# Row maxima of self attention: joined per 128 queries and sent by transfers of 4-byte pieces, in place of a transpose per block

## The reference, cut to what matters

```python
scores = jnp.einsum('bqhd,bkhd->bhqk', q, k) / np.sqrt(HD)
attn = jax.nn.softmax(scores.astype(jnp.float32), axis=-1)
out = jnp.einsum('bhqk,bkhd->bqhd', attn, v)
```

## Time and profile before

| | us |
|---|---|
| median of 3 runs | 3796.76 (3792.34 to 3797.68) |
| the profiled execution, its own time | 3797.3 |
| its span in the trace | 3795.5 |

### The profile page before, as it was taken

The page is one execution under the profiler, slowest core; times in us unless marked ns, Lnnn a source line. Parts: engine busy times, 40 slices in busy tenths (PEclk is TensorE's granted clock), DMA queues, the critical chain, the costliest instruction groups (busy, mean ns, idle before and its releaser), DMA issues.

```text
span 3795.5 us, 59346 instructions
## 1 busy us (share of the span) xinstructions
PE 3443.8 (91%) x22289; PEld 2023.6 (53%) x22289; DVE 2237.3 (59%) x3533; ACT 2316.6 (61%) x4047; POOL 830.5 (22%) x546
## 2 busy tenths in 40 slices
PE   8999998898999888998898889988998899899988
PEld 6777776434644564446435744465446443564465
DVE  3323324885386556953885559636955487549654
ACT  2333333786577645875786557765874578657764
POOL 0322323003400521024003410051014100340051
PEclk8989989999999999999999999999999999999999
DMA  5001002000000001001000010000000100000000
GB/s 173 7 29 34 6 31 89 1 13 24 27 2 1 13 15 53 2 24 38 2 2 13 12 56 2 24 24 16 2 13 12 56 1 13 24 27 2 7 18 13
DMA packets 73089, 87.17 MB, mean 23 GB/s; under 512 B 11823, under 2 KB 62578, under 8 KB 72694
## 3 DMA queue, kind: packets, MB, share of 16 engines
q1 hardware_dynamic: 47846, 63.23, 5.1%
q10 hardware_dynamic: 24976, 20.15, 1.7%
HBM read 72.49 MB, written 9.56 MB: 22 GB/s over the span
## 4 chain that ended last, share of the span: by engine, by line
PE 76%; DVE 13%; ACT 7%; issue 2%; POOL 1%; DMA 0%; SPq 0%; ACTq 0%; DVEq 0%; POOLq 0%
PE ps L677 71%; DVE mxh L1721 4%; ACT probs L1406 3%; PE ps L1122 3%; DVE ctxk L1670 2%; DVE ow L1746 1%; PE ps L983 1%; DVE tok L1456 1%; DVE x L1687 1%; DVE small L1440 1%; DVE mx L1718 1%; ACT qs L1373 1%; POOL hidl L1832 1%; POOL small L1768 1%; ACT ow L1412 1%
## 5 line engine op out<-in xcount | busy, mean ns | idle before, releaser
L1406 ACT ACTIVATE probs<-ps 128x512 f32<-128x512 f32 (+1 forms) x2176 | 1216.5, 638 | 290.3 <-PE ps L677 247.7
L1721 DVE TENSOR_REDUCE mxh<-ps 128x2 f32<-128x1024 f32 x1024 | 1212.7, 1220 | 155.8 <-PE ps L677 152.7
L677 PE MATMUL ps<-probs,v 128*32 128x256 f32 (+2 forms) x7616 | 727.9, 454 | 6.3 <-ACT probs L1406 6.3
L677 PE MATMUL ps<-ks,qs 64*128 64x512 f32 x2048 | 483.1, 480 | 63.7 <-DVE mxh L1721 45.3
L1768 POOL TENSOR_TENSOR small<-small 128x4 f32<-128x4 f32 x66 | 67.8, 1027 | 2012.8 <-DVE small L1450 2012.8
L677 PE MATMUL ps<-qs,ks 64*128 64x512 f32 x2048 | 455.6, 425 | 4.0 <-DVE mxh L1721 2.5
L677 PEld LDWEIGHTS ps<-ks,qs 64*128 64x128 f32 x2048 | 192.8, 183 | 424.8 <-issue 302.0
L677 PEld LDWEIGHTS ps<-qs,ks 64*128 64x128 f32 x2048 | 248.1, 186 | 184.1 <-ACT probs L1406 150.1
L677 PEld LDWEIGHTS ps<-probs,v 128*32 128x32 f32 (+1 forms) x7616 | 150.2, 108 | 275.8 <-ACT probs L1406 204.6
L677 PE MATMUL ps<-hT,slot 128*128 128x512 f32 x448 | 233.5, 654 | 21.8 <-issue 8.5
L1718 DVE TENSOR_REDUCE mx<-ps 128x4 f32<-128x312 f32 x384 | 166.2, 478 | 146.2 <-PE ps L677 142.8
(11 more groups left out here) (221 smaller groups left out, 5919.2 us busy)
## 6 DMA issues: line engine op xcount, KB each, us to landing
slot<-in_L_w SPq DMA_DIRECT2D x8, 1024.0 KB, 10.0
slot<-in_L_fc_w SPq DMA_DIRECT2D x8, 1024.0 KB, 5.4
xin<-in_x ACTq DMA_DIRECT2D x5, 1024.0 KB, 6.1
x_after_block<-x ACTq DMA_DIRECT2D x20, 256.0 KB, 2.4
xin<-x_after_block SPq DMA_DIRECT2D x5, 1024.0 KB, 5.5
ew<-in_L_e_w SPq DMA_DIRECT2D x6, 768.0 KB, 14.3
x<-in_x ACTq DMA_DIRECT2D x4, 1024.0 KB, 6.9
qs<-mrow SPq DMA_DIRECT2D x256, 2.0 KB
```

The lines of the kernel that those rows point to most:

```text
L677: return pe.matmul(out, lhsT, rhs, start=start, stop=stop)
L1406: ins = act.activation(dst, src, ACT.Exp, scale=SCALE)
L1721: dve.tensor_reduce(mxh[:, z, t, j // 2, j % 2, :], ps[:, a:a + 2, :], AX.X, ALU.max, negate=True).then_inc(dve_done, M.add(dve_done, name))
```

## The change

The join now works on one query block: `both` has a step for each t, with 128x4 results in place of 128x16, and stands one A behind the last reduction of its t. Behind each join SP waits for it and issues four transfers, one per head, which take one column of `mx` (128 partitions, 4 bytes each) to 512 consecutive bytes of one partition of `qs`. The transpose M, ScalarE's copy and the four transfers of 512-byte runs are kept for the first block (0, 0) of each module only, and dropped for the other seven. The joins of the third block wait for the kept M, and from the fourth block on a block's first join waits for the transfers of the block two before it (they read the same half of `mx`); ScalarE's wait for transfers goes. Wait counts on `maxima_stacked` grow with the number of transfers.

```diff
     def self_attention(tag, follow):
-        maxima, turn = [], []
+        maxima, last = [], []
         for g in range(GROUPS):
             for n in range(NH):
-                scores = [("A", g, n, t, j) for t in range(TPH) for j in range(GH)]
-
-                behind = 1 if (g, n) == (0, 1) else 4
-                maxima += turn[:1] + scores[:behind] + turn[1:] + scores[behind:]
-                turn = [("both", g, n), ("M", g, n)]
-        maxima += turn
+                for t in range(TPH):
+                    maxima += [("A", g, n, t, 0)] + last + [("A", g, n, t, j) for j in range(1, GH)]
+                    last = [("both", g, n, t)]
+                if (g, n) == (0, 0):
+                    maxima += last
+                    last = [("M", g, n)]
+        maxima += last
...
+                        if KIND[tag] == "self" and (g, n) != (0, 0):
+                            for t in range(TPH):
+                                sp.wait_ge(dve_done, upto(dve_done, (tag, "both", g, n, t)))
+                                at_column = n * HALF + t * P
+                                for j in range(GH):
+                                    sp.dma_start(qs[stacked(j % 2, MAXROW, MAXROW + 1), 2 * g + j // 2, at_column:at_column + P].bitcast(F32),
+                                                 mx[:, z, 0, TPH * j + t:TPH * j + t + 1]
+                                                 ).then_inc(maxima_stacked[g][n], M.add(maxima_stacked[g][n], (tag, j - GH + 2) if t == TPH - 1 else None, LOADED))
+                            continue
...
-                        if not cross and NH * g + n >= 2:
-                            act.wait_ge(maxima_stacked[g - 1][n], upto(maxima_stacked[g - 1][n], (tag, 1)))
...
-                        g, n = step[1:]
+                        g, n, t = step[1:]
                         z = maxima_of(tag, g, n)[0]
-                        if NH * g + n >= 2:
-                            dve.wait_ge(mm_done, upto(mm_done, (tag, "M", g - 1, n)))
-                        dve.wait_ge(dve_done, upto(dve_done, (tag, "A", g, n, TPH - 1, GH - 1)))
-                        dve.tensor_tensor(mx[:, z, 0, :].rearrange("p (c e t) -> p t c e", t=TPH, e=2), mxh[:, z, :, :, 0, :], mxh[:, z, :, :, 1, :], ALU.min
-                                          ).then_inc(dve_done, M.add(dve_done, (tag, "both", g, n)))
+                        if (g, n) == (1, 0):
+                            dve.wait_ge(mm_done, upto(mm_done, (tag, "M", 0, 0)))
+                        elif NH * g + n > 2 and t == 0:
+                            dve.wait_ge(maxima_stacked[g - 1][n], upto(maxima_stacked[g - 1][n], (tag, 1)))
+                        dve.wait_ge(dve_done, upto(dve_done, (tag, "A", g, n, t, GH - 1)))
+                        dve.tensor_tensor(mx[:, z, 0, :].rearrange("p (c e t) -> p t c e", t=TPH, e=2)[:, t], mxh[:, z, t, :, 0, :], mxh[:, z, t, :, 1, :], ALU.min
+                                          ).then_inc(dve_done, M.add(dve_done, (tag, "both", g, n, t)))
```

More of the change, by code:

```diff
@@ L1062, in _ @@
                         pe.wait_ge(act_done, upto(act_done, *act_was))
-                        last = (tag, "A", GROUPS - 1, n, TPH - 1, 0) if cross else (tag, "both", g, n)
+                        last = (tag, "A", GROUPS - 1, n, TPH - 1, 0) if cross else (tag, "both", g, n, TPH - 1)
                         pe.wait_ge(dve_done, upto(dve_done, last, *dve_was))
```

## The result

The change made the kernel slower: 3806.09 us, median of 20 runs (3791.15 to 3811.55), against 3792.39 for the kernel before in the same comparison. The ratio is 1.0038, with a 95% interval of 1.0027 to 1.0050. One of the 20 executions of the kernel before took 6517.69 us and is left out of the ratio; the others took 3781.46 to 3797.73. The forecast was 3764 us and faster, with a range that ended at 3779, so size, range and sign were all wrong. The changed kernel's profiled execution took 3810.91 us with a span of 3809.0, which is 13.5 us more than the span before, at a mean granted TensorE clock of 0.956 where before had 0.961.

The account below looks back on a forecast made before the run. TensorE was taken as the bound, busy 91%. Per module 2.6 + 1.8 - 0.3 = 4.1 us, times 8 modules 32.8 us, off the profiled 3797.3 gave 3764.5, forecast as 3764 us; range 3754 to 3779.

Parts of the forecast that it names:

- Added: joins on VectorE: Four joins per block in place of one: hidden in the stream, 0.3 us per module ahead of it, bounds 0 and 0.8.
- Removed, in the stream: Six transposes between later A matmuls go: 0.43 us each, 2.6 us per module, bounds 1.3 and 2.6.
- Removed, at the end: The transpose behind the last A and its join goes: S comes earlier, 1.8 us per module, bounds 0 and 2.27.
- Transfers: 112 new transfers replace 28 per module: SP keeps up, issue and landing hidden, 0.9 us in hand at the last block.
- rival (a): The last block's transfers land late and take back the end's 1.8 us: 3778 us; chance 0.13 with other part losses.
- 4-byte pieces: Each t sends 512 pieces into one or two partitions; needs 10.2 ns or less each, 8.3 taken, so nearly free.
- rival (c): Pieces into one partition above 10.2 ns delay each block's first S: 3845 to 4135 us; chance 0.08 with anything else slower.
- (b): VectorE becomes the bound in the stream if a join costs 0.35 us or more: near 3796 us; chance 0.05 with (d).
- (d): ScalarE's exponentials hold the cycle, so removing the transposes saves no time: time unchanged; chance 0.05 with (b).

Follow-up runs that it names:

- e1: The changed kernel with each join as a minimum reduction with one SBUF operand in place of two: 3734.97 us, ratio 0.9861 to the kernel before.
- e2: The changed kernel, two-operand joins kept, with GpSimd's addition waiting for the first block's last join: 3734.24 us, ratio 0.9857 to the kernel before.
- e4: The changed kernel with each module's first block joined as a whole again, behind its last reduction: 3742.42 us, ratio 0.9885 to the kernel before.
- e3: The kernel before with three extra two-operand joins in each module's first block, their results written again by the old join: 3834.08 us, ratio 1.0125.
- e9: The changed kernel plus 19 unread matmuls per module where TensorE idled behind the held join: 3776.47 us, ratio 0.9971 to the kernel before.
- e6: e1 with the six transposes inside the stream and ScalarE's copies put back as dead work: 3770.52 us, ratio 0.9951 to the kernel before.
- e7: e1 with only the last block's transpose put back, as dead work: 3764.98 us, ratio 0.9941 to the kernel before.
- e5: The changed kernel, two-operand joins kept, with GpSimd's addition in self attention cut into four pieces: 3753.77 us, ratio 0.9912 to the kernel before.
- e8: e1 with the first block also sent by 4-byte transfers, so no transpose in self attention: 3743.87 us, ratio 0.9885 to the kernel before.
- e10: e2 with three GpSimd memsets of x beside the second block's join in the four L1 self attentions: 3752.87 us in one run.

## Why the prediction was wrong, step by step

**The step that failed: "Added: joins on VectorE".** It took 0.10 us for each new join and 0.3 us per module for the lead, with bounds of 0 and 0.8. It measured 5.9, 47.5 us in eight modules. The price came from the earlier trace rows, where the one join stands at 689.14, behind GpSimd's addition (in the trace of before it runs from 680.47 to 685.04). The new join of t = 1 stands at 680.9, inside it. I priced an instruction by its row and moved it to another place without asking what the other engines do there: the addition's row stands in the trace of the kernel before, and no step of the prediction uses it; the earlier trace rows says POOL 0.00 only for the blocks. e1, e2 and e4 take the meeting away in three ways and all end 1.1 to 1.4% below the kernel before; e3 puts it into the kernel before and loses 1.2%. The Trainium skill (SBUF — State Buffer, Who interferes with whom) has this rule: a VectorE instruction with two SBUF inputs contends with a GpSimd instruction that reads SBUF, not with one that only writes, and the later of the two waits for the earlier to finish; tensor_reduce does not contend on this chip. The traces agree on every count: 4.00 us beside the addition, 1.06 beside the subtraction, 0.16 beside the memsets, 0.15 as a reduction.

**A term that was missing: the clock.** The bounds held nothing for an idle TensorE. Of the 5.9 us, 2.0 came after the stall, with matmuls at the lower clock, and e9 got 1.87 of it back in the lead.

**Removed, in the stream: right.** 0.43 each was taken, 21.42 - 20.97 = 0.45 measured, and e6 puts it back with the transposes. In the changed kernel itself three of the eight modules lost part of it again to a lower granted clock: the stretch from the first exponential to the last reduction takes 145.9 to 146.1 us in five modules and 147.2 to 149.6 in the other three.

**Removed, at the end: right in mechanism, too small by 1.2 us per module.** 1.8 us per module was taken. In the first module the changed kernel's chain ran 3.25 us behind that of the kernel before in the last of the blocks with A (its exponentials end at 838.35 against 835.10), at the S behind the last A only 1.62 (844.95 against 843.33): a gain of 1.63, and e7 measures 1.60. Over the eight modules the gain is 24.0 us, 3.0 each. The transpose cost 1.7 where the clock stayed at 1.00, but in six modules of the kernel before the granted clock fell behind the 1.92 us in which TensorE waited for the join, and there it cost 2.9 to 4.3. The same stretch ran below 1.00 in all eight modules of e3, which has this transpose, and in one of e7's; in the nine kernels without it (the changed one and e1, e2, e4, e5, e6, e8, e9, e10) it took 27.5 us in every module. So the low clock comes only with this transpose, but not always; what decides it is not shown. What is late next was named rightly: S waits 0.34 us for a bank, as a reduction frees it.

**Transfers: right.** An issue takes 0.60 us, where 0.4 to 0.6 was expected, the landing 2.0 where 1.63 was taken, and no S waited for one. So rival (a) did not occur. Behind the last A the chain is on TensorE for the next 10.91 us without a break.

**4-byte pieces: right.** 512 pieces per t, at intervals of 5.2 us, made no S late, so a piece costs less than 10.2 ns, and rival (c) did not occur. A transfer of 128 pieces landed 2.0 us after its issue, one of four pieces 1.63: 0.37 us for 124 more pieces, as an estimate 3 ns each. By the minimum of about 10.5 ns a packet that the Trainium skill states for loads from HBM (DMA: Bandwidth & Descriptors, Measured) it would be, as an estimate, 1.3 us; these rows don't show it.

**Rivals (b) and (d)** needed a period of 21.4 and are excluded by 20.97, though VectorE is now busy for 58.63 us of the 62 of the stretch in the earlier trace rows, 1.27 more.

The chance of 0.08 for slower was given to the pieces of 4 bytes; no rival named what happened. The trace was read closely in the blocks, where the gain was, and on VectorE alone in the lead, where the added work met something new.

**Where the rest lies.** With the meeting gone the forecast of 3764 should have held, and e1 and e2 came out near 3735: 53 us gained, where the lead's 0.1 and the two gains of the first module count 34. Split by module, the profiled executions of the kernel before and e1 differ by 44.3 us in the self attentions: 19.8 in the blocks (2.6 x 8 = 20.8 was taken), 24.0 at the end (14.4 was taken), and 0.5 in the lead and ahead of it. The table has this for every kernel, as its difference to the kernel before in us (its self attentions take 1656.6 us in all, the rest 2138.9, of which 666.2 lie ahead of the first):

| | in the eight self attentions | outside | of that, ahead of the first | medians |
|---|---|---|---|---|
| changed | +11.3 | +2.3 | -0.1 | +13.7 |
| e1 | -44.3 | -18.3 | -8.7 | -53.0 |
| e2 | -44.3 | -9.4 | 0.0 | -53.7 |
| e3 | +50.8 | -11.0 | -3.9 | +46.1 |
| e4 | -44.6 | -10.3 | -4.5 | -45.6 |
| e5 | -29.6 | -3.2 | -5.2 | -33.8 |
| e6 | -24.0 | -1.8 | -11.3 | -17.0 |
| e7 | -30.3 | -22.9 | -16.6 | -22.5 |
| e8 | -45.5 | -11.4 | -8.6 | -43.7 |
| e9 | +6.1 | -19.5 | -16.4 | -14.8 |
| e10 (one run) | -41.2 | -3.3 | +0.2 | -38.4 |

The medians follow the first column to within 10 us, with e9 as the exception (21). The edit changes no instruction outside, so what is seen there is not the work that it adds or removes. The work ahead of the first self attention, 3008 matmuls in each trace, took 666.2 us at a mean granted clock of 0.92 in the kernel before and 649.8 at 0.94 in e9. An example further on: the kernel before has

```profile
1322.02:1382.24 60.22, 55.47 (x336) 44.72 (x334) 35.62 (x61) 25.00 (x47) 22.34 (x19) 0.91 0.06 18
```

and e1, for the same work,

```profile
1303.42:1361.24 57.82, 52.71 (x337) 43.13 (x336) 35.61 (x61) 25.05 (x47) 22.38 (x18) 0.97 0.06 19
```

so 2.4 us less with a granted clock 0.06 higher.

**What stays open.** Why the clock of untouched stretches differs from one trace to the next was not tried, nor whether it goes with the kernel or only with the execution; the runs of one kernel spread by some 17 us (before 3781 to 3798). So differences under about 10 us between two of these kernels say little, and e9's 25 us are not explained. Also open is why e5 and e9 lose some of their gain to a low clock behind the lead, which e1 and e2 do not.

## What to carry to other kernels

Before a two-operand VectorE instruction is added or moved, read GpSimd's timeline at the place where it will stand: beside a GpSimd instruction that reads SBUF it can cost that instruction's whole rest, here 4 us in place of 0.15. A form with one SBUF operand, or a wait that puts GpSimd's work elsewhere, avoids it; with either (e1, e2) this change is worth 1.4% and beats both kernels, where as written it loses 0.4%. A stall that lets TensorE run empty is to be priced with the slower matmuls behind it, here half as much again. And an account is to be added up over all repetitions of a module: the first one times eight gave the right total here, though the parts of the other seven were different.

## What the runs showed of the hardware

- A two-operand VectorE instruction on 4 values per partition was held for 4.00 us by a GpSimd addition that reads SBUF and ended with it; one with a single operand took 0.15 us beside the same addition, and three GpSimd memsets did not hold the two-operand one (0.16 us, one run).
- The held time is recorded as VectorE's busy time, with no waiting shown. The sign of it is a longest duration far above the median (3999 ns against 156) whose end is the end of a GpSimd instruction.
- After 4.54 us of idle TensorE the granted clock was 0.50 for the next 5.8 us; with matmuls in the idle stretch it stayed at 1.00 there and the lead was 1.87 us shorter, but 14 matmuls further on took 4.53 us in place of 3.17.
- A wait of 1.92 us of TensorE ahead of a transpose was followed by a stretch of some 30 us at a mean granted clock of 0.94 or 0.89 in six of eight modules of the kernel before, and at 1.00 in the other two. Without the transpose it was 1.00 in 72 modules of nine kernels.
- A transfer of 128 pieces of 4 bytes from 128 partitions into one took 0.60 us to issue and 2.0 us to land, against 0.57 and 1.63 us for four pieces of 512 bytes.
